# The merge of attention heads in a three-block transformer kernel: a new layout for the z scratch, another order of the loads, and two tiles of x1 loaded early

## What is computed

```python
x = x + xattn(layernorm(x), ...)   # cross attention, one head, 256 + 64 keys
x = x + attn(layernorm(x), ...)    # 16 heads of 128, rotary, causal
x = x + ffn(layernorm(x), ...)     # 4-bit weights, 1408 hidden, RMS norm of the output
```

```python
z = einsum('bnqk,bknd->bqnd', probs, V)
out = einsum('bqnd,ndm->bqm', z, W_O) + b_O          # summed over 16 heads
...
vals = FP4_LUT[nib].reshape(out_f, in_p * 8)          # weights of the third block, unpacked
```

## Time and profile before

| | |
|---|---|
| median of 3 runs | 1428.65 us |
| the profiled execution | 1427.44 us |
| its span, first to last instruction | 1425.6 us |
| TensorE busy | 1357.8 us, 95% |
| VectorE busy | 976.7 us, 69% |
| ScalarE busy | 507.8 us, 36% |
| GpSimd busy | 429.1 us, 30% |
| mean granted TensorE clock | 0.985 |

### The profile page before, as it was taken

The page is one execution under the profiler, slowest core; times in us unless marked ns, Lnnn a source line. Parts: engine busy times, 40 slices in busy tenths (PEclk is TensorE's granted clock), DMA queues, the critical chain, the costliest instruction groups (busy, mean ns, idle before and its releaser), DMA issues. The chain is left out here.

```text
span 1425.6 us, 23392 instructions
## 1 busy us (share of the span) xinstructions
PE 1357.8 (95%) x8964; PEld 792.5 (56%) x8964; DVE 976.7 (69%) x2176; ACT 507.8 (36%) x1249; POOL 429.1 (30%) x302
## 2 busy tenths in 40 slices
PE   8999999958999999999999999999699999999998
PEld 6666666425666666666667666654244434343433
DVE  6444444447887788778877778727698596969693
ACT  3222223322333333333333333310001474838281
POOL 0000000003333233333333333320323291919192
PEclk9999999988999999999999999999899999999999
DMA  8555555332001100101010000277831000000000
GB/s 327 212 207 210 206 195 198 148 107 74 16 31 60 60 31 31 60 16 60 31 60 31 31 25 22 89 219 173 201 123 60 1 1 30 0 30 0 29 1 30
DMA packets 59451, 122.42 MB, mean 86 GB/s; under 512 B 4312, under 2 KB 37720, under 8 KB 52696
## 3 DMA queue, kind: packets, MB, share of 16 engines
q1 hardware_dynamic: 59080, 118.19, 24.3%
q10 hardware_dynamic: 272, 2.88, 0.9%
HBM read 95.89 MB, written 25.17 MB: 85 GB/s over the span
## 5 line engine op out<-in xcount | busy, mean ns | idle before, releaser
L925 POOL TENSOR_TENSOR hd_rotated<-hd_products 64x512 f32<-64x512 f32 x64 | 113.0, 1766 | 708.1 <-DVE hd_products L1109 708.1
L184 PE MATMUL psum<-hd_xt_hi,hqk_hi 128*128 128x512 f16 x512 | 194.8, 381 | 1.6 <-DVE hd_xt_lo L1083 1.6
L185 PE MATMUL psum<-hd_xt_lo,hqk_hi 128*128 128x512 f16 x512 | 194.4, 380 | 0.0
L186 PE MATMUL psum<-hd_xt_hi,hqk_lo 128*128 128x512 f16 x512 | 194.3, 379 | 0.0
L1429 POOL TENSOR_TENSOR ff_part<-ff_part 128x512 f32<-128x512 f32 x88 | 127.7, 1467 | 107.2 <-DVE ff_part L1556 106.8
L184 PE MATMUL psum<-hd_wv_hi,hd_xt_hi 128*128 128x256 f16 x512 | 140.3, 274 | 5.2 <-DVE hd_wv_lo L1088 5.2
L1458 PE MATMUL psum<-ff_xt_hi,gu 128*128 128x512 f16 x352 | 133.9, 380 | 9.1 <-DVE w_rows L1594 3.3
L185 PE MATMUL psum<-hd_wv_lo,hd_xt_hi 128*128 128x256 f16 x512 | 140.2, 274 | 0.0
L186 PE MATMUL psum<-hd_wv_hi,hd_xt_lo 128*128 128x256 f16 x512 | 140.1, 274 | 0.0
L1459 PE MATMUL psum<-ff_xt_lo,gu 128*128 128x512 f16 x352 | 133.4, 379 | 0.0
L1556 DVE SCALAR_TENSOR_TENSOR ff_part<-psum,gu_scale,ff_part 128x512 f32<-128x512 f32 x176 | 119.7, 737 | 6.3 <-ACT ff_part L1506 3.6
(11 more groups left out here) (170 smaller groups left out, 2789.8 us busy)
## 6 DMA issues: line engine op xcount, KB each, us to landing
xa_kv_t<-in_ctx_t_dram SPq DMA_DIRECT2D x16, 1024.0 KB, 5.7
xa_kv<-in_ctx_dram SPq DMA_DIRECT2D x16, 1024.0 KB, 4.8
w_rows<-in_head_weights_dram SPq DMA_DIRECT2D x12, 1024.0 KB, 7.9
z_scratch<-hd_z_hi SPq DMA_DIRECT2D x32, 256.0 KB, 2.2
z_scratch<-hd_z_lo SPq DMA_DIRECT2D x32, 256.0 KB, 2.5
w_rows<-z_scratch SPq DMA_DIRECT2D x8, 1024.0 KB, 8.4
hqk_lo<-z_scratch SPq DMA_DIRECT2D x8, 1024.0 KB, 8.2
xn<-in_x_dram SPq DMA_DIRECT2D x8, 512.0 KB, 3.5
```

What stands on the lines that cost most here:

```text
L184: pe.matmul(out, lh, rh, start=(first and i == 0), stop=False)
L185: pe.matmul(out, lh, rl, start=False, stop=False)
L186: last = pe.matmul(out, ll, rh, start=False, stop=(final and i == k - 1))
L925: pool.tensor_tensor(rotated[0:HALF, w, 0, :], products[0:HALF, w, 0, :], products[0:HALF, w, 2, :], ALU.subtract)
```

## The change

The z scratch gets the shape (2, NT, 2, DH, HEADS // 2, TILE), so that one half tile of one part is contiguous and has 8 KB per partition. Stores follow it (runs of 2 KB). In the last attention step x1 of tiles 0 and 1 are both loaded, after the codes. In `merge_phase` SyncE issues z first after each wait; x1 of tile 2 follows z of tile 1 half 1, the down codes and scales follow z of tile 2 half 0, x1 of tile 3 follows z of tile 2 half 1. x1 of tiles 2 and 3 have a semaphore each, and GpSimd waits for each tile's x1 by itself (tiles 0 and 1 together).

```diff
 def z_of(z_scratch, hi_or_lo, half, t):
-    n = HEADS // 2
-    return z_scratch[hi_or_lo, half * n:(half + 1) * n, :, bass.ds(t * TILE, TILE)].rearrange("h d t -> d h t")
+    return z_scratch[hi_or_lo, t, half, :, :, :]
...
-                sp.dma_start(early.x2[:, 0:TT, :], rows_of(0)).then_inc(early_sems.x1_loaded, 16)
                 sp.dma_start(early.b_o, b_o.broadcast_to([P, D])).then_inc(early_sems.b_loaded, 16)
...
                 sp.dma_start(early.codes, codes_of(gu_codes, 0)).then_inc(early_sems.codes_loaded, 16)
+                for t in range(2):
+                    sp.dma_start(early.x2[:, t * TT:(t + 1) * TT, :], rows_of(t * TILE)).then_inc(early_sems.x1_loaded, 16)
...
-                    sp.dma_start(z_scratch[half, s.pair * 2:s.pair * 2 + 2, :, s.first_token:s.first_token + TILE].rearrange("h d t -> d h t"),
-                                 z[:, :, :]).then_inc(small_loaded_z_stored, 16)
+                    n = 2 * s.pair % (HEADS // 2)
+                    sp.dma_start(z_scratch[half, s.t, 2 * s.pair // (HEADS // 2), :, n:n + 2, :], z[:, :, :]).then_inc(small_loaded_z_stored, 16)
...
             load_z(1, 0)
             sp.dma_start(codes[1], codes_of(gu_codes, 1)).then_inc(gu_loaded[1], 16)
-            load_x1(1)
-            sp.wait_ge(z_used[1], 1)
-            load_z(1, 1)
-            for t in range(2, NT):
-                load_x1(t)
...
-            for t in range(2, NT):
-                if t == NT - 1:
-                    sp.wait_ge(z_stored, 16 * (HEADS_SMALL + 2 * NT * PAIRS))
-                for half in range(2):
-                    sp.wait_ge(z_used[half], t - 1 + half)
-                    load_z(t, half)
+            for t in range(1, NT - 1):
+                sp.wait_ge(z_used[1], t)
+                load_z(t, 1)
+                load_x1(t + 1)
+                if t == NT - 2:
+                    sp.wait_ge(z_stored, 16 * (HEADS_SMALL + 2 * NT * PAIRS))
+                sp.wait_ge(z_used[0], t)
+                load_z(t + 1, 0)
+                if t == 1:
+                    load_down()
+            sp.wait_ge(z_used[1], NT - 1)
+            load_z(NT - 1, 1)
...
-            pool.wait_ge(early_sems.x1_loaded, 16)
             for b in range(NT * TT):
-                if b == TT:
-                    pool.wait_ge(x1_loaded, 16 * (NT - 1))
+                if b == 0:
+                    pool.wait_ge(early_sems.x1_loaded, 32)
+                if b % TT == 0 and b >= 2 * TT:
+                    pool.wait_ge(x1_loaded[b // TT], 16)
...
-    z = nc.dram_tensor("z_scratch", (2, HEADS, DH, TOK), F16).ap()
+    z = nc.dram_tensor("z_scratch", (2, NT, 2, DH, HEADS // 2, TILE), F16).ap()
```

More of the change, by code:

```diff
@@ L836, in __init__ @@
                 self.a, self.t, self.pair, self.next_pair = a, t, pair, (pair + 1) % PAIRS
-                self.first_token = t * TILE
                 self.turn_next, self.att, self.proj = turn_next, att, proj
@@ L1204, in merge_phase @@
         hi_done, lo_done, value_ready = sem("hi_done"), sem("lo_done"), sem("value_ready")
-        x1_loaded, x1_ready = sem("x1_loaded"), sem("x1_ready")
+        x1_loaded, x1_ready = {t: sem(f"x1_{t}_loaded") for t in range(2, NT)}, sem("x1_ready")
         z_loaded = [sem("z0_loaded"), sem("z1_loaded")]
@@ L1229, in load_z, with load_down @@
                     sp.dma_start(z, z_of(z_scratch, hi_or_lo, half, t)).then_inc(z_loaded[half], 16)
+            def load_down():
+                sp.dma_start(down_c[:, 0, :], down_codes[0:WHOLE, :]).then_inc(down_loaded, 16)
+                for g in range(8):
+                    sp.dma_start(down_scale[16 * g:16 * g + 16, 0, :], down_scales[g:g + 1, :].broadcast_to([16, D])).then_inc(down_loaded, 16)
+                for q in range(REST):
+                    words = down_codes[WHOLE + 16 * q:WHOLE + 16 * q + 16, :]
+                    sp.dma_start(down_c[:, 1 + q, :], words.unsqueeze(0).broadcast_to([8, 16, D])).then_inc(down_loaded, 16)
+                    sp.dma_start(down_scale[:, 1 + q, :], down_scales[8 + q:9 + q, :].broadcast_to([P, D])).then_inc(down_loaded, 16)
@@ L1231, in load_x1 @@
             def load_x1(t):
                 sp.dma_start(x2[:, t * TT:(t + 1) * TT, :],
-                             x1_rows[t * TILE:(t + 1) * TILE, :].rearrange("(b p) d -> p b d", p=P)).then_inc(x1_loaded, 16)
+                             x1_rows[t * TILE:(t + 1) * TILE, :].rearrange("(b p) d -> p b d", p=P)).then_inc(x1_loaded[t], 16)
             load_z(1, 0)
             sp.dma_start(codes[1], codes_of(gu_codes, 1)).then_inc(gu_loaded[1], 16)
-            load_x1(1)
-            sp.wait_ge(z_used[1], 1)
```

## The result

The changed kernel takes 1415.59 us (median of 6 runs, 1409.87 to 1418.11), the kernel before 1428.63 us (6 runs, 1425.41 to 1430.76). The ratio is 0.9906, with a 95% interval of 0.9884 to 0.9928. It is faster, by 13.0 us where 21.0 were forecast, and it lies 1.1 us above the stated range. The profiled execution took 1416.11 us, its span is 1414.3.

A forecast was written before the change was run, and what follows sets the result against it. The merge was taken as bound by TensorE, with two stalls for z and slow clock behind them: 14.4 + 1.4 + 3.5 + 1.7 = 21.0 us. Removing these takes 1428.65 to 1407.7 us, range 1406.2 to 1414.5.

The forecast's parts named there:

- Where TensorE loses 21.0 us: In the merge: two stalls waiting for z, 14.4 and 3.5 us, and slow clock behind each, 1.4 and 1.7 us.
- Tile 1 half 1: z load in the merge: lands between 983.8 and 996.2, needed at 996.7, so its 14.4 us stall goes.
- Tile 2 half 0: z load in the merge: lands 1004.0 to 1020.0, needed at 1017.4; no stall taken, 2.6 plus 1.7 us kept.
- Rival 1: In the merge z still waits for the codes: 1411 to 1413 us, 1417 at the upper bounds; chance 0.16.
- Rival 2: z loads aren't made in 8 KB runs and only the order works: 1414 us; chance 0.05.
- Rival 3: z's new reads are moved by few DMA engines, 2 MB in 18 us, making it slower: 1439 us; chance 0.03.
- Rival 4: Stalls only move, to VectorE beside GpSimd or SyncE held past 955.2; within 0.2% of before; chance 0.02.
- GpSimd's three groups: In the merge: GpSimd's additions come in groups of 8, 4 and 4, VectorE's instructions beside them three to four times longer.
- the wait for the first codes: At the merge's opening: VectorE's 3.94 us wait goes, since the codes come before the block opens.
- The reading of 19.8 us as the landing of z's high part: Kernel before, tile 1 half 1: z's high part needed 19.8 us beside the codes, against 5.4 alone.
- the argument against turns of whole packets: If engines drained whole packets per ring, 1 KB runs would pass the codes almost as if alone; 19.8 us speak against it.
- The layout's worth: z in 8 KB rows: half tile 7.3 instead of 8.3 us, that 1 us hidden; an eighth of the runs matters.

The follow-up runs named there:

- down_later: Changed kernel with the 15 loads of down codes and scales issued after x1 of tile 3, some 20 us later: 1414.11 us, ratio 0.9906.
- x1_last: Changed kernel with x1 of tile 2 issued behind the down loads: 1408.42 us, ratio 0.9869.
- codes_short_rows: Changed kernel with each load of codes made as 4 broadcasts of a quarter of the columns, rows of 2816 instead of 11264 bytes: 1408.43 us, ratio 0.9866.
- codes16: Changed kernel with each load of codes made as 8 DMAs of 16 partitions instead of one broadcast: 1408.09 us, ratio 0.9858.
- short_rows_x1_last: Changed kernel with codes in rows of 2816 bytes and x1 of tile 2 behind the down loads: 1405.15 us, ratio 0.9841.
- layout_only: Kernel before with the new z scratch alone, SyncE's order and x1 as before: 1425.48 us, ratio 0.9991.

## Why the prediction was wrong

- **Where TensorE loses 21.0 us** was right: kernels without its two stalls take 1405 to 1408.4 us, where the forecast was 1407.7. What the prediction describes is reached by other kernels than this one.
- **Tile 1 half 1** was right: forecast 983.8 to 996.2, complete at 989.6. Its room is thin, though: of some 20.2 us it took 17.7 in the changed kernel run again, 18.1 and 20.4 in `down_later` and `x1_last`, and 29.4 with x1 in rows of 8 KB.
- **Tile 2 half 0 is the step that failed.** It had a span of 1004.0 to 1020.0 for a need at 1017.4, took no stall and kept 2.6 + 1.7 us. It was complete at 1024.5, or 1022.6 counted from the merge's opening as forecast, 2.6 beyond the upper bound. The mis-sized term is x1 of tile 2: priced at 3.6 us, the time of a tile of x1 with the engines to itself, it was in flight 35.8 us. Tile 1 half 1 was ahead of it until 989.6; after that it took turns with the long rows of codes 2 and 3. Moving it away took the wait away (`x1_last`). The codes were under-priced too: 12.4 us in the sum, 21.2 and 25.6 us from issue to landing for groups 2 and 3. What was sized by adding up prices of transfers alone is a shared queue, in which a short row costs its own time and that of the neighbour's long row. The text had this mechanism ("if runs of one queue alternate with the big ones of the other") and used it for z only.
- **Rival 1** came true in kind (z waits for the codes), at the second of its two places, with 7.8 us in the profile; its 0.16 looks too small, and its upper case of 1417 should have been in the range, since "0.5 us of room at the worst" and an upper bound beyond the need both spoke for it.
- **Rival 2** (8 KB rows not made) is out: the page of the profile counts 28120 transfers under 8 KB after and 52696 before. Rival 3 is out: both loads of z in these rows were complete after 11.2 us here and after 7.6 us in `codes_short_rows`, where it had 18. Rival 4 is out: VectorE ended the gate and up pieces at 1039.2, 82.0 us after the opening, forecast 86.4; SyncE issued its last DMA of the heads phase at 949.0, 8 us before the opening.
- **GpSimd's three groups**, 8, 4 and 4, and VectorE's waits in the last blocks are as forecast. So is the wait for the first codes, nearly: 0.6 instead of 3.9 us. The first group of additions began at 963.16, 1.9 us later than forecast when counted from the opening, and nothing waited for it.
- **The reading of 19.8 us as the landing of z's high part** in the kernel before was not safe: it is the sixteenth of 32 arrivals of both parts. The high part can't have been complete before that, so the argument against turns of whole packets stands.
- **The layout's worth** was half seen: the rows count, not the 1 us of bandwidth. But it was called decisive for the first stall by itself, and it isn't: alone it gave 0.9991.

## What to carry to other kernels

When loads share the DMA engines, don't add up the times they take alone: list what is in flight beside each, with the length of its rows. Where two queues share engines, what is needed first should have long rows, and what is not urgent short ones; here cutting four bulk loads into rows a quarter as long gave as much as reordering. Put a load that nobody waits for behind the one that is waited for, even where it looks small, and take a bound that reaches past the time of need as a case, not as a reserve.

## What was not expected of the hardware

- Rows of SyncE's and of ScalarE's queue take turns one for one: 60 of 2 KB against 60 of 11 KB in 6 us, 66 of 1 KB against 66 of 11 KB in 8 us. A semaphore's increment of 4 bytes counts as a turn: 150 against 76 and 76 in `codes16`. At the start of a load this did not hold (46 against 139 in `short_rows_x1_last`).
- A transfer that is in flight on all engines can be nearly done on some and late on others: x1 of tile 2 in the changed kernel had 8 of its 16 arrivals at 992.2 and the last at 1014.7, and z of tile 2 half 0, issued at 998.7 behind it, had 16 of 32 at 1012.1. The last 16 came at 1018.7 to 1024.5.
- Many rows outstanding hold the issuing engine: 14.06 us in z's issues before the change, 0.80 us in the same issues when `layout_only` had z in 8 KB rows. There, and in the changed kernel, the hold came later, 37.42 and 11.95 us in the issue of small scale loads. What is queued behind on SyncE waits with them; z of tile 2 half 1 was issued 2.8 us late for it (1022.09, its place free at 1019.3), without consequence.
